# A four-layer graph network on one core: one exponent step per pair, variance steps on GpSimd, weight loads ordered by use, new orders of all engines

## What is computed

```python
def reference(x, adj, ...):
    x = _layernorm(x + _L0_gnn_ref(x, adj, W, a_src, a_dst))   # attention
    x = _layernorm(x + _L1_gnn_ref(x, adj, W, a))              # attention
    x = _layernorm(x + _L2_gnn_ref(x, adj, a0, ..., bias))     # sigmoid of scores
    x = _layernorm(x + _L3_gnn_ref(x, adj3, adj, weight, bias))# sum over neighbours
    return x
# layers 0 and 1
    h = einsum('bnf,of->bno', x, W)
    e = leaky_relu((h @ a_src)[:, :, None] + (h @ a_dst)[:, None, :])
    alpha = softmax(where(adj == 0, -big, e), axis=-1)
    return einsum('bij,bjo->bio', alpha, h)
```

## Time and profile before

| | us |
|---|---|
| device time, median of 3 runs | 265.18 (264.46 to 265.67) |
| the profiled execution, device time | 264.89 |
| its span in the profile | 263.1 |
| granted TensorE clock, mean | 0.969 |

### The profile page before, as it was taken

The page is one execution under the profiler, slowest core; times in us unless marked ns, Lnnn a source line. Parts: engine busy times, 40 slices in busy tenths (PEclk is TensorE's granted clock), DMA queues, the critical chain, the costliest instruction groups (busy, mean ns, idle before and its releaser), DMA issues. The chain is left out here.

```text
span 263.1 us, 5911 instructions
## 1 busy us (share of the span) xinstructions
PE 233.2 (89%) x1761; PEld 210.0 (80%) x1761; DVE 227.1 (86%) x834; ACT 230.6 (88%) x743; POOL 128.2 (49%) x163
## 2 busy tenths in 40 slices
PE   7498998899997998999999999999999969789840
PEld 7477878789886987999989899988999868778630
DVE  0647988999989999999999999999999898998860
ACT  1069999999999999999999989999949978998971
POOL 1000212333636476548468452947446753777960
PEclk9869999999999999999999999999999998999995
DMA  6955835224301313221212031010011000010122
GB/s 204 396 173 191 252 125 189 94 80 162 94 29 45 118 42 121 81 80 44 80 42 81 2 100 61 4 39 21 24 42 40 0 4 1 0 41 2 41 81 87
DMA packets 12147, 21.79 MB, mean 83 GB/s; under 512 B 1104, under 2 KB 5968, under 8 KB 12112
## 3 DMA queue, kind: packets, MB, share of 16 engines
q1 hardware_dynamic: 11264, 20.98, 24.0%
q10 hardware_dynamic: 848, 0.40, 0.5%
HBM read 17.17 MB, written 4.19 MB: 81 GB/s over the span
## 5 line engine op out<-in xcount | busy, mean ns | idle before, releaser
L531 POOL TENSOR_TENSOR frstd<-fvar,minus_half 128x4 f32<-128x4 f32 x64 | 65.1, 1021 | 98.6 <-ACT fvar L674 71.0
L1164 PE MATMUL banks<-vals_all,wgt_all 128*128 128x129 f32 x512 | 63.6, 277 | 1.1 <-DVE fres L890 0.5
L1164 PEld LDWEIGHTS banks<-vals_all,wgt_all 128*128 128x128 f32 x512 | 59.9, 191 | 2.8 <-issue 0.9
L526 POOL TENSOR_TENSOR xb<-xs_all,bias_cen 128x256 f32<-128x256 f32 x64 | 45.3, 727 | 23.9 <-ACT xs_all L665 13.5
L848 DVE SCALAR_TENSOR_TENSOR wgt_all<-banks,gain,mask_all 128x256 f32<-128x256 f32 x128 | 52.3, 471 | 0.0
L898 DVE BATCH_NORM_STATS2 fstats<-fres 128x6 f32<-128x256 f32 x128 | 47.9, 415 | 0.0
L668 ACT ACTIVATE xs_all<-fres,frstd 128x128 f32<-128x128 f32 x124 | 40.6, 448 | 2.0 <-POOL frstd L531 2.0
L1164 PE MATMUL banks<-xs_all,wgt_all 128*128 128x128 f32 x256 | 33.0, 284 | 1.1 <-DVE wgt_all L856 1.0
L1164 PEld LDWEIGHTS banks<-xs_all,wgt_all 128*128 128x128 f32 x256 | 31.1, 199 | 2.2 <-issue 1.8
L1131 PE MATMUL banks<-fxT,fxTa 128*128 128x256 f32 x128 | 30.9, 385 | 2.0 <-DVE fstats L898 1.6
L665 ACT ACTIVATE xs_all<-fres,fcenter,frstd 128x128 f32<-128x128 f32 x64 | 27.0, 550 | 1.5 <-DVE fcenter L912 1.5
(11 more groups left out here) (89 smaller groups left out, 423.5 us busy)
## 6 DMA issues: line engine op xcount, KB each, us to landing
adj_all<-adj_turned SPq DMA_DIRECT2D x16, 512.0 KB, 3.7
xT_all<-x_turned SPq DMA_DIRECT2D x16, 256.0 KB, 2.7
x_all<-x_laid SPq DMA_DIRECT2D x16, 256.0 KB, 3.1
out<-xs_all SPq DMA_DIRECT2D x16, 256.0 KB, 2.2
bias<-biases_laid ACTq DMA_DIRECT2D x1, 128.0 KB, 7.6
...
w_fast<-W_turned ACTq DMA_DIRECT2D x1, 64.0 KB, 3.5
w_nat<-in_L_gnn_W ACTq DMA_DIRECT2D x1, 64.0 KB, 5.0
```

What stands on the lines that cost most here:

```text
L526: nc.gpsimd.tensor_tensor(xb(u)[:, :, :], xs(u)[:, :, :], bias_cen[:, int(l) - 2, :, :], ALU.add).then_inc(fast_pool[k], 1)
L531: nc.gpsimd.tensor_tensor(frstd[:, int(l), slot(n), :], fvar[:, int(l), slot(n), :], minus_half[:, :, :], ALU.pow).then_inc(fast_pool[k], 1)
L1164: last = nc.tensor.matmul(place(f"out{l}", u)[:, b * width:(b + 1) * width], wgt(u)[:, c, b * P:(b + 1) * P], (vals if l in "01" else xs)( ...
```

## The change

- `v` (`exponentials`): one 128x4 exponent step per pair with one largest logit for the pair, instead of two 128x2 steps with one each. `dmax` reduces 4 values to 1 instead of 2.
- 28 of the 48 variance steps of layers 0, 2 and 3 stand in GpSimd's list (10 of `var0`, 9 of `var2`, 9 of `var3`). Before, ScalarE had 46 and VectorE 2, now ScalarE has 20 and VectorE none. All but one stand directly ahead of their own `pow`.
- `norm3` of pairs 10 and 11 goes from ScalarE to VectorE, `bias3:14` from GpSimd to VectorE, `low:14` from VectorE to GpSimd.
- The loads of the layer 1 weights, the layer 3 weights and the biases leave ScalarE's queue and become `weights` steps of SP, behind the first ten loads of pairs.
- The masks of pairs 2 and 7 are VectorE's instead of those of 0 and 11.
- `score` now also waits for `xT2` by name, which stands ahead of `xTa` on the same engine anyway.
- 5 idle products instead of 13. `turn:0` and the `centre` steps come later.
- All `ORDER` strings and all `BANKS` are new. `scale_xTa` and `normalize` of GpSimd are new functions that no step uses.

```diff
 "sp": (
-        "xT:0 x:0 xT:1 adj:0 x:2 xT:2 x:1 adj:1 adj:2 x:3 xT:3 adj:3 xT:4 adj:4 xT:5 x:4 adj:5 adj:6 xT:6 x:5 adj:7 x:6 "
+        "xT:0 adj:0 xT:1 adj:1 xT:2 adj:2 x:0 adj:3 x:1 x:3 weights:0 x:2 xT:3 weights:2 weights:1 xT:4 adj:4 xT:5 "
 "pe": (
-        "turn:0 h0:0 dT0:0 rows0:0 top0:0 h0:1 dT0:1 rows0:1 top0:1 h0:2 out0:0 dT0:2 rows0:2 top0:2 xT1:0 out0:1 h1:0 "
+        "h0:0 dT0:0 h0:1 rows0:0 top0:0 dT0:1 rows0:1 h0:2 out0:0 rows0:2 top0:1 dT0:2 xT1:0 top0:2 out0:1 h0:3 out0:2 "
...
-        minus_dmax = sb("minus_dmax", [P, B])
+        minus_dmax = sb("minus_dmax", [P, TEAMS])
...
+            def load_weights(l, n, k):
+                dst, src, signal = ((w1_nat[:, :], W1, w1_in), (w3[:, 0, :], W3[0], weights_in), (bias[:, :, 0, :], biases_laid, biases_in))[n]
+                sp.dma_start(dst, src).then_inc(signal, 16)
...
-            act.dma_start(w1_nat[:, :], W1).then_inc(w1_in, 16)
-            act.dma_start(w3[:, 0, :], W3[0]).then_inc(weights_in, 16)
-            act.dma_start(bias[:, :, 0, :], biases_laid).then_inc(biases_in, 16)
...
-                for u in graphs(n):
-                    last = nc.scalar.activation(vals(u)[:, :, D], logit[:, int(l), u, :, 1], ACT.Exp, bias=minus_dmax[:, u:u + 1])
-                last.then_inc(fast_act[k], 1)
+                nc.scalar.activation(vals_all[:, pair(n, VALS), :, D], logit[:, int(l), slot(n), :, 1], ACT.Exp, bias=minus_dmax[:, n:n + 1]).then_inc(fast_act[k], 1)
...
-                nc.vector.tensor_reduce(minus_dmax[:, slot(n)], place(f"h{l}", n * H)[:, 400:400 + H * NB].rearrange("p (u b) -> p u b", b=NB), AX.X, ALU.max,
-                                        negate=True).then_inc(fast_dve[k], 1)
+                nc.vector.tensor_reduce(minus_dmax[:, n:n + 1], place(f"h{l}", n * H)[:, 400:400 + H * NB], AX.X, ALU.max, negate=True).then_inc(fast_dve[k], 1)
...
-            idle_products(9)
+            idle_products(5)
             projection_columns()
-            idle_products(4)
```

More of the change, by code:

```diff
@@ L537, in low_part, with normalize, scale_xTa @@
                     nc.gpsimd.tensor_tensor(lo(u)[:, :, :], xs(u)[:, :, :], hi(u)[:, :, :], ALU.subtract).then_inc(fast_pool[k], 1)
+            def normalize(l, n, k):
+                pool.wait_ge(fast_dve[k], at("dve", "center1", n * H))
+                if n >= XS:
+                    pool.wait_ge(fast_stored[n % XS], 16 * (n // XS))
+                for u in graphs(n):
+                    for b in range(NB):
+                        last = nc.gpsimd.tensor_scalar(xs(u)[:, b, :], fres(u)[:, b, :], frstd[:, 1, u, b:b + 1], fcenter[:, u, b:b + 1], ALU.mult, ALU.add)
+                    last.then_inc(fast_pool[k], 1)
+            def scale_xTa(l, n, k):
+                if n == first("pool", "xTa"):
+                    pool.wait_ge(w0_in, 16)
+                if n >= FXTA:
+                    pool.wait_ge(fast_pe[(n - FXTA) % K], at("pe", "agg", final(n - FXTA)))
+                for u in graphs(n):
+                    pool.wait_ge(fast_act[k], at("act", "xT2", u))
+                    nc.gpsimd.tensor_scalar(fxTa(u)[:, :], fxT(u)[:, :], a2[:, 0:1], None, ALU.mult).then_inc(fast_pool[k], 1)
             def residual(l, n, k):
@@ L555, in scales @@
                 nc.gpsimd.tensor_tensor(fscale[:, slot(n), :], vals_all[:, pair(n, VALS), :, D], frstd[:, 0, slot(n), :], ALU.mult).then_inc(fast_pool[k], 1)
-            steps = {"bias": biases, "pow": powers, "low": low_part, "res": residual, "var": variances, "fscale": scales}
+            steps = {"bias": biases, "pow": powers, "low": low_part, "res": residual, "var": variances, "fscale": scales, "xTa": scale_xTa, "norm": normalize}
             for step, l, n in order("pool"):
@@ L1060, in _ @@
                         "rows1": (fast_dve, "dve", "weight1"), "out1": (fast_dve, "dve", "res1"),
-                        "xT2": (fast_act, "act", "xTa"), "score": (fast_dve, "dve", "alpha"),
+                        "score": (fast_dve, "dve", "alpha"),
                         "agg": (fast_act, "act", "agg")}
```

11 lines of the change are left out of this document (7 added, 4 removed), and 194 rows, old and new, of tables (BANKS, ORDER).

## The result

The changed kernel takes 261.6 us, the median of 4 runs (260.2 to 262.7), against 265.4 for the kernel before (264.5 to 265.7): 3.8 us between the medians. The ratios and the times of the experiments leave out executions more than 1.5% above the fastest of their kernel, among them two of the kernel before at 789 us and two of e11 at 579 us, whose cause is open. The forecast was 256.5 us, 8.7 less than the 265.2 it knew, in a range of 250.0 to 263.5. So the direction was right and the time lies in the range, but less than half of the forecast gain came. The profiled execution took 260.24 us. It is the fastest of the four, and its span is 258.2 us.

The account below looks back on a forecast made before the run. No engine alone bound the kernel; ScalarE did from 21.3 to 150 us, others hardly less loaded. On VectorE, 228.7 busy plus 9.5, 7.0, 9.2 idle and 1.8 outside gave 256.2, forecast as 256.5 us, range 250.0 to 263.5.

Parts of the forecast that it names:

- the sum: Whole kernel, made on VectorE: 228.7 us busy plus 9.5, 7.0 and 9.2 idle give a span of 254.4 us.
- rival 3: At the end GpSimd binds, busy 45 to 50 us from 200 to 250, chains 4 us longer: 260.5 us; 8%.
- So the middle should look like the stretch from 150 to 200 us all along: Middle: with ScalarE some 16 us below VectorE in work, VectorE would be idle only 2% throughout.
- the 7.0 us that follow: VectorE's idle time between first `rsum` and drain: 7.0 us instead of 13.7, so 6.7 us gained.
- Rival 1: Middle: waits only change their cause, TensorE taking ScalarE's part; VectorE's idle time stays 13.7 us, time 263.2 us; 17%.
- The start. 3.7 us gained: Fill: first `rsum` at about 15.5 us instead of 21.3, VectorE's idle time until then 9.5 us instead of 13.2.
- Rival 4: Fill: TensorE stays at its lower clock, perhaps until 30 us, adding 12 us: 268.5 us, slower than before; 5%.
- The prediction's own sign of being wrong: TensorE's granted clock at 0.50 beyond 20 us, or VectorE's and TensorE's waits staying as long although ScalarE is relieved.
- ScalarE's relief: ScalarE's work falls by 8.6 (exponents), 6.8 (variance steps) and 2.6 us (`norm3`), from 230.6 to 212.6 us.
- The norm steps on VectorE: Two `norm3` pairs moved from ScalarE add 2.9 us to VectorE, at 1.43 us a pair.
- The 8 us: Upper bound for the two moved `norm3` pairs if a GpSimd `pow` of 1.02 us held every instruction; 2.9 was kept.
- The 1.0 us that was taken off: VectorE's busy time: 1.0 us less because `rinv`, `res` and `umax`, `alpha` follow each other immediately less often.

Follow-up runs that it names:

- e11: The kernel before with only the 28 variance steps moved to GpSimd, still two exponents per pair: 262.9 us, ratio 0.9963.
- e1: The kernel before, old orders, with one exponent per pair and the 28 variance steps on GpSimd: 261.8 us, ratio 0.9875.
- e3: The changed kernel with idle products added in three places where TensorE waits in the fill: 259.6 us, ratio 0.9801.
- e10: The kernel before with one exponent per pair, 28 variance steps on GpSimd and 12 idle products ahead of `dT0:0`: 258.2 us, ratio 0.9788.
- e6: The changed kernel with less VectorE work, the row statistics reading 96 of 128 features: 259.5 us, ratio 0.9807.
- e12: The changed kernel with three cuts: `seen` reads one graph of two, statistics 96 of 128 features, `agg` the high parts alone: 257.0 us, ratio 0.9724.
- e2: The changed kernel with two exponent instructions per pair again, all else as in the change: 264.0 us, ratio 0.9967.
- e7: The changed kernel with less TensorE work, `agg` of layer 3 multiplying the high parts alone, 64 matmuls less: 260.8 us, ratio 0.9830.

## Why the prediction was right and wrong

Where the time of the sum went, as VectorE's idle time, from the windows of each kernel:

| | span | to 25 us | 25 to 200 | 200 to drain | last 13.1 us | busy |
|---|---|---|---|---|---|---|
| before | 263.1 | 13.3 | 8.4 | 5.1 | 9.2 | 227.1 |
| change | 258.2 | 11.4 | 5.4 | 3.2 | 9.2 | 228.9 |
| e1 | 259.5 | 13.7 | 5.8 | 4.8 | 7.6 | 227.6 |
| e3 | 257.0 | 10.4 | 5.5 | 3.2 | 9.4 | 228.5 |
| e10 | 257.9 | 11.9 | 6.1 | 4.7 | 7.6 | 227.6 |
| e6 | 255.8 | 10.8 | 10.5 | 4.0 | 9.8 | 220.7 |
| e12 | 255.7 | 11.8 | 9.4 | 4.7 | 9.3 | 220.5 |

**Right.** The first `logits` (7.00 us) and the first `rsum` (14.63, forecast 15.5), VectorE's busy time (228.9, forecast 228.7, in part by luck, see below), its idle time up to the first `rsum` (9.1 and 9.5) and in the drain (9.2 and 9.2). A variance step on GpSimd took 196 ns, nearer the low end, as taken. The waits for `pow` at the end didn't grow: the `norm` group waited 1.5 us for it in all, against 2.0, so rival 3 didn't happen. From 25 to 150 us VectorE idles 2.2%, the 2% that was forecast.

**Wrong: the step "So the middle should look like the stretch from 150 to 200 us all along" and the 7.0 us that follow.** Measured 10.9. Some 2.1 us of the excess lie between 14.6 and 25 us, where 2% was assumed and 22% measured. Some 1.9 lie between 25 and 200: the stretch from 150 to 200 itself went from 1.9% to 5.2%. Its small idle time had been no property of the stretch. It was what the old order left on VectorE there: in the old orders it idles 1.0, 0.6 and 1.0 us (before, e1, e11), in the new ones 2.6 and 3.0 (the change, e2), with one exponent or two. e6 and e12 show what is wrong with such a sum at its root: of 8.2 to 8.4 us taken off VectorE, 5.8 and 5.9 came back as its idle time (29.3 to 35.1 and 35.2 us). Busy time and idle time of an engine that is one of three aren't two terms that can be estimated apart. Rival 1 (the waits only change their cause, 263.2) came nearest to this mechanism, with 17%, and was nearer the time (261.6) than the forecast; but its term was 13.7 us, and the middle lies half way between. That TensorE in particular takes ScalarE's part, as it said, isn't shown: e7, the cut on TensorE, gave 1.6 us, uncertain by as much.

**Wrong: "The start. 3.7 us gained".** It was right up to the first `rsum` (4.0) and half gone at 25 us. The walk stopped at the first `rsum`, and behind it the second `out0` ran at the lower clock. Rival 4 had this mechanism, but with a price of 12 us for a clock that stays low until 30 us; it was low for 3.4 us and e3 prices it at 2.4. The prediction's own sign of being wrong, a granted clock of 0.50 beyond 20 us, came true here. As to the time, e1 has the old start and the old orders and is as fast as the change (-3.3 and -2.9, within the uncertainty). So in the time nothing is seen of the earlier start and the new orders together. The price of the first `h0` at the lower pace (2.10 us) came true.

**Wrong in size: ScalarE's relief.** 18.0 us by group busy times, 9.5 by the engine's total. It changed the forecast little, because the sum was made on VectorE, but it made ScalarE's slack look like 16 us where it was 8 (228.9 and 221.0). With two exponents again, in e2, ScalarE's share of the chain is back at 33%. The list of waits in the prediction also left out that VectorE waited for ScalarE itself from 21.3 to 250 us, 2.1 us at L811 and 1.1 at L837. In the change 0.8 us and nothing are left of these, so this part of the relief came.

**The norm steps on VectorE** were taken at 1.43 us a pair for the two new pairs. The three pairs on VectorE took 1.43, 0.87 and 0.90; one of the 12 instructions was held. The new steps thus added 1.8 us and not 2.9. All of them on line L820 of the changed kernel, least, median and most in ns:

```profile
L820 DVE TENSOR_SCALAR xs_all<-fres,frstd x12: 274/282/840, 69.2 to 233.5; 128x128 f32<-128x128 f32 x12
```

The hold stands at 69.82 us, where GpSimd ran the addition of the same pair's first graph:

```profile
69.85 0.72 POOL L530 TENSOR_TENSOR xb<-xs_all,bias_cen 128x256 f32<-128x256 f32 x1 [2.29 <-DVE xs_all L820]
```

The 8 us that the exclusive lock of the Trainium skill (SBUF — State Buffer, Who interferes with whom) could have cost at most did not come. The rule agrees with this one hold. It doesn't agree with the pair at 225.91 us: a `pow` ran from 225.23 to 226.24 beside its first two instructions, and they took 284 and 296 ns. There the measurement decides: in this trace no `pow` held a normalization.

Other steps of VectorE were held by these additions, which the sum left out. The 16 `var1` steps (L919, the old L904) took 139 to 728 ns in the changed kernel, median 163, and 134 to 164 before. Two of them took 0.73 us, at 113.09 and 168.19, while GpSimd ran additions of 128x256. By groups `var1` has 1.6 us more than before. So VectorE's busy time came out as forecast in part by luck: the norm steps cost less than assumed, and these held steps made up for it. The 1.0 us that was taken off for `rinv` and `res` in succession was no busy time either: in the trace before, `rinv` ends at 21.81 us and `res` starts at 21.92, so the gap is idle.

**The median** was taken 0.3 us above the profiled execution; it was 1.35, and 2.0 instead of 1.8 us lay outside the span. Of the 5.1 us between forecast and result, 3.8 are the span, 0.2 lie outside it and 1.1 are this step.

**What the gain is, then.** ScalarE's relief gives it (e1), at some 0.4 us for each us by which its busy time fell (222.9 us in e1, 7.6 less). The new orders with the earlier start add nothing that can be measured (e1 against the change, e11 against e2). Keeping TensorE at its full clock in the fill gives nearly as much again in either order (e3, e10). The best version seen is e10 at 258.2 us, 2.1% under the kernel before: the old orders, one exponent per pair, 28 variance steps on GpSimd and 12 idle products.
